# A graph kernel whose gathers go from straight-line code into a loop, with the node numbers in a ring

## The reference, cut to what matters

```python
xw = x @ W.T
edge_feat = b_inv[:, None] * segment_sum(xw[src], he)     # sum of gathered rows, by group
out = d_inv[:, None] * segment_sum(edge_feat[he], src) + b
```

## Time and profile before

| what | us |
| --- | --- |
| median of 3 runs (range) | 7698.47 (7685.65 to 7712.91) |
| the profiled execution | 7689.32, its span 7687.6 |
| POOL busy in the span | 4404.5 |
| PE busy in the span | 4515.9 |
| DVE busy in the span | 2714.4 |
| pass 1, first gather to last | 1215.5 |
| pass 2 | 1204.8 |
| pass 3 | 1187.5 |
| pass 4 | 1210.3 |

### The profile page before, as it was taken

The page is one execution under the profiler, slowest core; times in us unless marked ns, Lnnn a source line. Parts: engine busy times, 40 slices in busy tenths (PEclk is TensorE's granted clock), DMA queues, the critical chain, the costliest instruction groups (busy, mean ns, idle before and its releaser), DMA issues. The chain is left out here.

```text
span 7687.6 us, 79625 instructions
## 1 busy us (share of the span) xinstructions
PE 4515.9 (59%) x19412; PEld 3521.9 (46%) x19412; DVE 2714.4 (35%) x7400; ACT 995.3 (13%) x2969; POOL 4404.5 (57%) x4603
## 2 busy tenths in 40 slices
PE   3555555555555555555445444499963666666579
PEld 2434443444444443344333333399942444444368
DVE  3111111222222111111244444422275666666544
ACT  0001001000000000000000000143331000000233
POOL 4666665666666566666666666411135666665345
PEclk8777777777777777776777777799976777777689
DMA  4333333333333333333344444307025444444345
GB/s 147 101 100 100 102 101 111 100 102 100 103 101 100 94 104 103 102 102 104 106 126 123 124 123 123 104 0 209 1 75 146 119 120 119 119 118 109 123 84 89
DMA packets 458800, 814.33 MB, mean 106 GB/s; under 512 B 93602, under 2 KB 316803, under 8 KB 458027
## 3 DMA queue, kind: packets, MB, share of 16 engines
q0 software_dynamic: 222080, 576.78, 27.9%
q1 hardware_dynamic: 235347, 226.08, 9.4%
q10 hardware_dynamic: 1208, 9.86, 0.3%
HBM read 649.02 MB, written 163.60 MB: 106 GB/s over the span
## 5 line engine op out<-in xcount | busy, mean ns | idle before, releaser
L371 POOL DMA_INDIRECT s_rows<-table,ids x2496 | 2378.2, 953 | 1290.3 <-issue 718.4
L638 PE MATMUL s_part<-s_rows,s_onehot 128*128 128x257 f32 x6656 | 2041.4, 454 | 770.6 <-issue 414.7
L638 PEld LDWEIGHTS s_part<-s_rows,s_onehot 128*128 128x128 f32 x6656 | 1507.9, 233 | 1167.7 <-issue 881.2
L1497 POOL DMA_INDIRECT at_rows<-h_t,ids x832 | 809.9, 973 | 471.9 <-issue 251.3
L475 DVE TENSOR_SCALAR s_inv<-s_raw 128x1 f32<-128x1 f32 x416 | 62.7, 151 | 2869.1 <-ACT s_raw L420 2274.1
L371 POOL DMA_INDIRECT s_rows<-xn_d,ids x832 | 788.7, 948 | 478.1 <-issue 239.3
L611 PE MATMUL s_psY<-w,s_xT 128*128 128x256 f32 x832 | 299.1, 495 | 809.0 <-ACT s_y L404 523.6
L1902 PE MATMUL at_part<-at_rows,at_onehot 128*128 128x264 f32 x1664 | 612.9, 499 | 4.0 <-DVE at_onehot L1719 4.0
L611 PEld LDWEIGHTS s_psY<-w,s_xT 128*128 128x128 f32 x832 | 192.5, 244 | 888.1 <-ACT s_xT L398 372.4
L524 DVE TENSOR_TENSOR s_onehot<-s_fixed,rel 128x1024 f32<-128x1024 f32 x416 | 508.6, 1223 | 170.5 <-issue 111.9
L420 ACT ACTIVATE s_raw<-s_part 128x257 f32<-128x257 f32 x416 | 159.7, 384 | 2012.8 <-DMA acc<-in_x 1063.6
(11 more groups left out here) (367 smaller groups left out, 5693.2 us busy)
## 6 DMA issues: line engine op xcount, KB each, us to landing
s_rows<-table,ids POOLq DMA_INDIRECT x2496
xs_d<-blank SPq DMA_DIRECT2D x38, 1032.0 KB
table<-s_y SPq DMA_DIRECT2D x208, 128.0 KB
ex_x<-xs_d SPq DMA_DIRECT2D x60, 258.0 KB, 3.4
s_rows<-xn_d,ids POOLq DMA_INDIRECT x832
table<-s_x SPq DMA_DIRECT2D x104, 128.0 KB
s_at_node<-in_x SPq DMA_DIRECT2D x104, 128.0 KB
s_at_node<-xn_d SPq DMA_DIRECT2D x104, 128.0 KB
```

The lines of the kernel that those rows point to most:

```text
L371: pool.indirect_dma_start(rows[:, t % RT, 0:D], None, table[0:NP_, :], bass.IndirectOffsetOnAxis(cst["ids"][:, t:t + 1], 0)).then_inc(rows ...
L638: ins = pe.matmul(part[u][:, 0:D + 1], onehot[:, u, t % JT, :], rows[:, t, 0:D + 1], start=False, stop=(t == JT * u + JT - 1))
L1497: pool.indirect_dma_start(rows[:, t % AHEAD, :], None, table, bass.IndirectOffsetOnAxis(cst["ids"][:, t:t + 1], 0)).then_inc(rows_in[t % A ...
```

## The change

POOL's 832 gathers become a loop of 26 rounds with 32 gathers each. In a loop the instruction's column of node numbers has to be a fixed one, so a ring `ids` of 32 columns (four parts of eight, one for each group of a round) is put between: DVE copies eight columns of `cst["ids"]` into a part of it and raises a new semaphore `ids_ready`. The first four parts are copied at the start of a pass. Part u gets the columns of group g+4 when `raw_ready` says that group g has been copied out of PSUM; the copy stands behind `one_group(g+3)` and ahead of `finish(g)`. POOL waits for it ahead of each group, behind its wait for `summed`. The loop over tiles in `tiles_alone` is rewritten to go by rounds, too.

```diff
+        ids = m.sb(f"{name}_ids", [P, RT], I32)
...
         @block.gpsimd
         def _(pool):
-            for t in range(NT):
-                if t % G4 == 0:
-                    pool.wait_ge(summed, t + G4)
-                    pool.sem_inc(issue, 1)
-                pool.indirect_dma_start(rows[:, t % RT, 0:D], None, table[0:NP_, :],
-                                        bass.IndirectOffsetOnAxis(cst["ids"][:, t:t + 1], 0)
-                                        ).then_inc(rows_in[t % RT // G4], 16)
+            with pool.Fori(0, ROUNDS) as i:
+                for t in range(RT):
+                    if t % G4 == 0:
+                        pool.wait_ge(summed, RT * i + t + G4)
+                        pool.sem_inc(issue, 1)
+                        pool.wait_ge(ids_ready, RG * i + t // G4 + 1)
+                        pool.sem_inc(issue, 1)
+                    pool.indirect_dma_start(rows[:, t, 0:D], None, table[0:NP_, :],
+                                            bass.IndirectOffsetOnAxis(ids[:, t:t + 1], 0)
+                                            ).then_inc(rows_in[t // G4], 16)
...
         @block.vector
         def _(dve):
+            def place_ids(g, u):
+                dve.tensor_copy(ids[:, JT * u:JT * u + JT], cst["ids"][:, bass.ds(JT * g, JT)]).then_inc(ids_ready, 1)
+
+            for u in range(RG):
+                place_ids(u, u)
             dve.sem_inc(scaled, 4)
...
                         if not last or u + LA < RG:
                             dve.wait_ge(raw_ready, g + LA + 1)
                             one_group(g + LA, u + LA)
+                        if not last:
+                            dve.wait_ge(raw_ready, g + 5)
+                            place_ids(g + RG, u)
                         finish(g, u)
```

More of the change, by code:

```diff
@@ L311, in stage_row_pass @@
         std_in, std_ready, x1_ready = m.sem(f"{name}_std_in"), m.sem(f"{name}_std_ready"), m.sem(f"{name}_x1_ready")
-        issue = m.sem(f"{name}_issue")
+        issue, ids_ready = m.sem(f"{name}_issue"), m.sem(f"{name}_ids_ready")
         alone_ready, alone_added, copied = (m.sem(f"{name}_{n}") for n in ("alone_ready", "alone_added", "copied"))
@@ L553, in tiles_alone, with tiles_of @@
                 dve.memset(acc[:], 0.0).then_inc(alone_added, 4)
[L554 to L559, removed]
+                def tiles_of(i, last):
+                    for k in range(RT):
+                        t, u = RT * i + k, k % 4
+                        if u == 0:
+                            first = nc.values_load_multi_w_load_instructions(
+                                cst["first"][0:1, 0, bass.ds(t, 4)], engines=[mybir.EngineType.DVE], min_val=0,
+                                max_val=NP_ - 1)[1]
                         dve.wait_ge(alone_added, t + 4)
@@ L566, in tiles_alone @@
                                           ).then_inc(alone_added, 1)
+                        if not last and k % JT == JT - 1:
+                            place_ids(RG * i + RG + k // JT, k // JT)
+                with dve.Fori(0, ROUNDS - 1) as i:
+                    tiles_of(i, False)
+                tiles_of(ROUNDS - 1, True)
                 dve.wait_ge(alone_added, NT + 4)
```

## The result

The changed kernel takes 7846.77 us in the median of 4 runs (7839.32 to 7858.18), the kernel before 7699.52: a ratio of 1.0196, 95% interval 1.0183 to 1.0209. It is 147 us slower. The forecast was 7860, with a range of 7710 to 7990.

A forecast was written before the change was run, and what follows sets the result against it. POOL's gathers and stops were taken to set the pace. Late boundaries 153.6 us, address steps 14 and pass starts 1 sum to 169 us, on 7689.3 profiled or the median: 7860 us; forecast bounds 7800 to 7900, range 7710 to 7990.

The forecast's parts named there:

- The loop costs nothing: POOL's 26 turns a pass: taken as 0 us, since turns run beside gathers; at most 28 us.
- Straight-line code costs nothing: Loading POOL's straight-line gathers: removing it was taken to gain 0 us, with -9 us as the bound.
- rival C: POOL's 81 "remote" stops, 349.9 us, are code coming in late; the loop ends them, about 7530 us; chance 0.08.
- 9 us of unexplained idle time: POOL's idle time above 0.305 us a gather that nothing explains, over the span; bound for code loading.
- A boundary is later by what stands between PE's release and the ring: POOL's new wait at group boundaries of the four passes: later starts at 142 boundaries, 153.6 us in sum.
- The delays add: Streaks after a stop keep 1.25 us a gather, so late starts in the passes are not made up.
- rival B: Delays in the passes are paid back as streaks grow to 32 gathers: 7694 us, no change; chance 0.13.
- lateness at boundaries: POOL's late starts in the four passes: 153.6 us at 142 boundaries, plus 14 us for address steps.
- The instruction with the short wait: DVE's line 516, read as waiting 0.44 us in the open against 2.70 us while gathers stream.
- Rival A: POOL caught in mid-streak: 29 further boundaries in pass 4 and 10 elsewhere become stops, about 7975 us; chance 0.19.
- The sign that the stops would be named after DVE's copy: In the changed trace, POOL's stops carry DVE's copy as name, each about 0.7 us longer in pass 3.
- The loop's branches fetch nothing: POOL's loop turns cause no fetch; the rival of 100 fetching turns, 160 us more, about 8000 us, had chance 0.03.

The follow-up runs named there:

- b1_wait_only: Kernel before with straight-line gathers on the full table, plus DVE's copies and POOL's wait for ids_ready; job with stops: 7908.08 us against 7761.42, ratio 1.0187.
- b2_ring_64: Changed kernel with a ring of 64 columns, numbers placed four groups earlier; job with stops: 7803.98 us against 7761.42 for the kernel before, ratio 1.0057.
- e1_wait_only: Kernel before with straight-line gathers, plus DVE's copies and POOL's wait for ids_ready; job without stops: 6800.03 us against 6808.19, ratio 0.9987.
- a2_before: The kernel before, unchanged, run again for its trace in a job with stops: 7689.15 us in a single run.
- c3_raw_first: Kernel before with ACT copying group g's sum ahead of the turned and multiplied results of groups g-2 and g-3; job without stops: ratio 0.9997.
- e2_ring_64: Changed kernel with a ring of 64 columns, numbers placed four groups earlier; job without stops: 6802.59 us against 6808.19 for the kernel before, ratio 0.9989.
- e4_copy_late: Changed kernel with DVE's copy moved behind finish(g); job without stops: 6810.46 us against 6808.19 for the kernel before, ratio 1.0003.

## Why the prediction was right

*The loop costs nothing*: right. With the ring in a loop and without (the first result, 1.0196, and `b1_wait_only`, 1.0187) the loss is the same within the intervals. In the changed kernel the gathers still follow each other at 0.305 us (237.0 us in 778 waits of pass 3), and so they do over the loop's turn: at the 75 turns of the four passes where POOL didn't stop the gap is 0.304 to 0.306 us.

*Straight-line code costs nothing*: right, and rival C is refuted. Leaving it out in the changed kernel won nothing, and bringing it back in `b1_wait_only` lost nothing. The "remote" stops were releases by PE that the profile couldn't place: 349.9 us under that name in the earlier trace rows, 14.8 us after the change, where the ring comes last, and 385.1 us in `b2_ring_64`, a loop with an early ring. The 9 us of unexplained idle time that the prediction took as the bound for the loading of code are the 6 stops of 1.88 us, and after the change there are more of them, not fewer.

*A boundary is later by what stands between PE's release and the ring*: right in kind, shown by the 0.81 us between copy and gather and by both ways of shortening the chain (the early ring, the wait for `summed`). In pass 3, 0.63 + 0.1 us was forecast for each of 25 stops; they grew by (173.6 - 151.4) / 25 = 0.89 us. The step before the copy is 0.11 us longer than line 475 had to wait, the copy 0.03, the handover 0.04, and POOL's silence before ACT's copies grew from 5.3 to 5.4 us.

*The delays add*: right in pass 3, where the streaks don't grow (24 streaks of 32 gathers before and after, as long as the buffer allows). In pass 4 it was too high, 87 against 69 us, and part of rival B is at work: before, it had 41 stops at group boundaries, of 4.2 us; after, 33 of 6.7 us, and all its streaks of 16 gathers have become 24. In pass 1 it was too high, too, 40 against 31 us, with 45 stops before and 40 after. In pass 2 it was too low (22 against 32); its stops went from 39 of 4.3 us to 35 of 5.5.

*That the sum fits so well is in part luck.* It has 168 us for lateness at boundaries, where the trace has 134. The 16 us of stops that are not at a boundary are in no term of the sum, and they make up for about half of the difference; 11 of them lie in pass 4, whose boundary stops alone grew by 53 us against the 87 forecast. The 47, 42 and 42 stops that the prediction counts include 6 of this kind. Without them the time would be about 7831 us by this count, still inside the range.

*Two readings of rows were off*, though the sum doesn't rest on them. The instruction with the short wait in the earlier trace rows, at 4302.00, doesn't stand in the open: POOL had been gathering again since 4297.16, and its fifth gather of that streak started at 4302.16. What the two lines show is that the slow waits set in some us after a stop, not with the first gather. And the boundaries of pass 3 that aren't late have 7.4 us or more to spare, not over 9.

*Rival A*, more boundaries that turn into stops: not in this kernel, where pass 4 has 33 of them instead of 41. In `b1_wait_only` it has 44, of which 11 follow streaks of 8, so the margin that A names is narrow; that its step on DVE makes these stops was not shown.

*The sign that the stops would be named after DVE's copy* came true in pass 1 (21 waits, 168.4 us, the pass's first gather among them) and in a part of pass 2; in pass 3 the name stayed PE's. The time between copy and gather shows it instead.

*The loop's branches fetch nothing*: right. POOL's loop adds 100 turns, and the changed page has 113 + 31 packets of instructions (q14 and q8), against 132 + 33 in the earlier trace rows and 143 + 32 in `b1_wait_only`, the same waits in straight-line code. The rule of the Trainium skill (page "Runtime: NRT & Kernel Launch", section "Instruction fetch mechanics") is about a taken branch whose target lies outside the window that was fetched; the packets show no such fetch for this body.

## What to carry to other kernels

A pacing engine that waits for one semaphore should not be given a second that is raised further down the chain, however cheap the instruction that raises it: its price is the length of that chain at each release for which it has to stand still, and here it was most of 147 us for 0.18 us copies that looked hidden. If the ring is wanted, fill it a full turn earlier: that took the cost from 1.9% to 0.6%. And time such an edit in more than one job, with the kernel before beside it and a look at whether its stops are there: the wait costs 1.9% in one job and nothing in the next.

## What the runs showed of the hardware

The jobs of these runs are of two kinds. The kernel before takes 7699 and 7761 us in two, 6808 and 6807 in two others, with the same work: POOL is busy for 4404.5 us in the first, 4408.2 (in `e1_wait_only`) in one of the others. In the slower kind the engines' own bookkeeping is at times held up while gathers stream. SP's address arithmetic ahead of its stores (min/median/max ns), in `a2_before` and then in `e1_wait_only`:

```profile
L349 SPq FUSED_REGOPS  x364: 3/37/1145, 115.3 to 4939.3; - x182
```

```profile
L350 SPq FUSED_REGOPS  x364: 37/37/42, 102.2 to 4284.2; - x182
```

The median is the same and the tail is not. It isn't the kernel: `c3_raw_first`, which is the kernel before but for ACT's order, has 37/37/42 as well. In the first profile of the kernel before, 33 of these 364 took over 0.1 us, and all 33 began while gathers followed each other. In its pass 3 no register instruction of any engine took over 0.3 us in the first 6 us of a streak (of 474), 80 of the 350 later ones did, and none of the 73 in a stop. ACT's copy comes 5.3 us after POOL fell silent there, about 3 to 4 us in the other passes (medians). What holds the engines up wasn't found; the runs show only that it goes with the job and not with the kernel. The chip number doesn't settle it, since number 7 had both kinds. All of POOL's stops in the four passes go with it, and so does the price of this change as far as it was measured: `e1_wait_only`, `e2_ring_64` and `e4_copy_late` cost nothing without stops, and the changed kernel itself wasn't run there.

Without stops the kernels with DVE's copy ahead of `finish` ran at 0.9985 to 0.9989 of the kernel before, each interval below 1; too little to matter, and not explained. What differs between the profiles is mostly the gathers' own time in the four passes: 3165.6 us in `e1_wait_only` (span 6797.0), 3175.8 in `c3_raw_first` (6808.4).
